# Linear attention mixed by node, graph marks in eight slots, weights and first batch norm ahead of their stages

## The chip, the cores and the metric

The kernel runs on one core of one Trainium2 chip. The metric is the device time of one execution in microseconds; lower is better. A core has five engines with an instruction queue each: TensorE (PE; PEld is its weight load), VectorE (DVE), ScalarE (ACT), GpSimd (POOL) and SyncE (SP, which here only starts DMAs). They are ordered against each other by semaphores alone. TensorE writes to eight PSUM banks of 128 x 512 f32; "bank" in a row is one of these, "arena" is the one SBUF tensor from which the kernel cuts all its tiles.

## The reference

A graph transformer of two layers on 1250 nodes with 512 features and 40000 edges. Cut to what matters here:

```python
xn = layernorm(x)
x = x + gnn0(xn, src, dst) + mix0(xn)        # layer 0; then experts
xn = layernorm(x)
x = x + gnn1(xn, edges) + mix1(xn)           # layer 1; then experts

# mix: linear attention, 8 heads of 64, no softmax
q, k, v = split(xn @ Wqkv)                   # mix1: Wqkv.T
q, k = elu(q) + 1, elu(k) + 1                # mix1: relu(q), relu(k)
kv = einsum('hnd,hne->hde', k, v)            # mix1: times temperature
den = einsum('hnd,hd->hn', q, k.sum(nodes)) + 1e-6     # mix1: max(.., 100)
y = (einsum('hnd,hde->hne', q, kv) / den) @ Wout + bout

# gnn0: three layers
for i in range(3):
    x = batchnorm(x) * gamma[i] + beta[i]    # over the nodes
    agg = segment_sum((x * src_norm)[src], dst) * dst_norm
    x = relu(agg @ W[i] + b[i])
```

All is f32. `src_norm` and `dst_norm` are inverse roots of the degrees, at least 1.

## The kernel before, in words

Nodes are cut into ten tiles of 125 (`NT`, `TS`), features into four blocks of 128 (`KT`). `st.turned` holds the normed features with features on the partitions (4 x 1250 columns), `st.res3` the residual with nodes on the partitions. The program is a list of stages; each is a block in which every engine has its own instruction list, with a barrier of all engines at its end. In layer 0 they are setup, layer norm, mixing, adjacency, graph, experts; in layer 1 layer norm, mixing, two rounds of attention on the graph, experts.

**Setup** (L112): edges and x are loaded by SP; VectorE makes from source and target two numbers for each edge: `st.low`, the place of the source in its tile, and `st.key`, target times ten plus the source's tile. `st.bound` has, for each window of 50 targets, the first and last group of four edge chunks that it needs.

**Layer norm** (L258): statistics on VectorE, root on ScalarE, scaling on VectorE, four transposes a tile on TensorE (L300), copy to `st.turned` on ScalarE. SP does nothing.

**Mixing** (`stage_mix`, L314, called once a layer; `relu` tells the second layer). SP loads the weights at its start. In layer 1 they come in rows and are turned, 16 blocks of 128 x 512, by TensorE (L395) and ScalarE (L464). Then keys and values of each node tile are made (L429, nodes on the PSUM partitions), VectorE and ScalarE shape the keys (L520, L479, L523), ScalarE copies the values (L474), and `kv_pair` (L410) adds keys times values, with a column of ones in the values that yields the sums of the keys. Queries are made the other way round, features on the partitions, in pieces of 500, 500 and 250 nodes (L425). Then for each of twelve pieces TensorE multiplies queries by the masked keys times values (L444) and by the spread sums (L445); VectorE takes the reciprocal of all of the latter (L556) and multiplies (L558). At last ten tiles are multiplied by the output weights (L454) and VectorE adds them to the residual (L563), behind the bias, which GpSimd adds to the residual (L385). In layer 0 GpSimd first makes `st.low_marks` (L382): for each of 320 chunks of 125 edges a 125 x 125 matrix in bf16 of zeros and ones; and VectorE takes the batch norm's statistics of the first graph layer (L498).

**Adjacency** (`stage_adjacency`, L572). For each of 25 windows, a loop with bounds in registers goes over its groups of four chunks: VectorE makes four marks of 125 x 500 in bf16 (L613) into four slots, TensorE multiplies each by the low marks (L637) into the window's bank, with one semaphore wait for each mark on both engines. ScalarE copies the counts (L647) and sums them. There are 104 groups. SP meanwhile zeroes two tables in memory.

**Graph** (`stage_graph`, L659). SP loads the first weights and the parameters; TensorE turns the latter (L768). For each layer the batch norm's moments (L721), root (L822) and factors (L724 to L730), the scaling of X in four pieces of 1250 columns (L733), ten products (L777), scaled by ScalarE (L825), then twelve aggregated pieces of 40 matmul records or fewer (L795), scaled (L752) and passed through relu (L834). Statistics of a feature block (L715) are taken once its three pieces are there.

## Time and profile before

| what | us |
|---|---|
| median of three runs | 2692.89 |
| lowest, highest | 2692.82, 2703.66 |
| the profiled execution | 2696.6 |
| its span, first to last instruction | 2694.8 |
| TensorE busy | 2270.1 |
| VectorE busy | 971.8 |
| ScalarE busy | 501.8 |
| GpSimd busy | 442.6 |
| mean granted TensorE clock | 0.935 |

The layer-0 stages, by the timeline: layer norm 27.1 to 43.3, mixing 43.5 to 271.8, adjacency to 457.6, graph to 871. The second mixing is at 1318.3 to 1542.4. How to read the rows below: in the busy time by stretch, a row has the stretch, its length, then for PE, PEld, DVE, ACT and POOL the busy time with the count of instructions, the granted TensorE clock (1.00 is 2.4 GHz, 0.50 is 1.2 GHz), the busy share of the DMA engines and GB/s. In the timeline a row has start, length, engine, line, operation, output <- inputs and shape, count of merged instructions, and in brackets how long the engine was idle before and what ended that. In the groups a row has the busy time, the mean length of one in ns, and the idle time before. An f32 matmul has two records.

### The profile page before, as it was taken

What the parts mean: (1) busy time and instruction counts of PE and PEld (TensorE: products, weight loads), DVE (VectorE), ACT (ScalarE), POOL (GpSimd) and SP (SyncE); (2) the same over time, 40 slices, a digit from 0 to 9 for tenths busy, and PEclk for the clock granted to TensorE, in tenths of its full rate; (3) what the DMA queues carried; (4) which work ended last, traced back from release to release, by engine and by line L of the source; (5) the groups of instructions that cost most, each with busy time, mean ns of one, the idle gap of its engine ahead of it and who ended that gap; (6) DMA issues with size and microseconds to landing.
All of it is one profiled execution on the core that took longest, in us unless ns stands there. A gap on an engine that the chain in (4) does not pass through costs nothing. (4 is left out here: it accounts for less than half of the span.)

```text
span 2694.8 us, 27626 instructions
## 1 busy us (share of the span) xinstructions
PE 2270.1 (84%) x7356; PEld 1284.5 (48%) x7357; DVE 971.8 (36%) x2322; ACT 501.8 (19%) x885; POOL 442.6 (16%) x599
## 2 busy tenths in 40 slices
PE   4976775989897898877498698998989988889996
PEld 2532332444444445444244246883458854435553
DVE  4162665420203632211105435531245402624443
ACT  1110122101010302222200014421134302201111
POOL 3995000000000014444100000000000010002332
PEclk9987998999999999999698898998999999989998
DMA  3000200000000326666300000002000010237774
GB/s 109 0 0 0 87 0 16 16 1 16 0 0 0 125 64 161 149 154 134 105 0 0 30 25 1 1 1 85 1 0 1 0 35 22 96 129 207 233 233 126
DMA packets 77350, 159.33 MB, mean 59 GB/s; under 512 B 9219, under 2 KB 20526, under 8 KB 77202
## 3 DMA queue, kind: packets, MB, share of 16 engines
q1 hardware_dynamic: 59602, 115.62, 12.8%
q0 software_dynamic: 17664, 42.64, 7.9%
q8 instruction: 47, 0.77, 0.1%
q14 instruction: 37, 0.30, 0.0%
HBM read 122.06 MB, written 38.74 MB: 60 GB/s over the span
## 5 line engine op out<-in xcount | busy, mean ns | idle before, releaser
L1692 PE MATMUL bank<-arena 125*125 125x257 f32 x1600 | 355.8, 383 | 4.8 <-DVE arena L1611 4.8
L1692 PEld LDWEIGHTS bank<-arena 125*125 125x125 f32 x1600 | 302.2, 189 | 60.5 <-DVE arena L1611 6.3
L1930 PE MATMUL bank<-arena 128*128 x832 | 250.9, 452 | 25.4 <-issue 12.6
L795 PE MATMUL bank<-arena 125*128 125x500 f32 (+1 forms) x720 | 252.6, 512 | 2.3 <-ACT arena L825 2.3
L1930 PEld LDWEIGHTS bank<-arena 128*128 128x128 f32 x832 | 157.0, 194 | 141.3 <-issue 81.8
L1507 PE MATMUL bank<-arena 128*125 128x512 f32 x480 | 211.3, 600 | 9.1 <-DMA arena<-in_L_gnn_W 9.1
L1948 PE MATMUL bank<-arena 128*128 x360 | 177.3, 622 | 36.3 <-ACT arena L1976 27.9
L795 PEld LDWEIGHTS bank<-arena 125*128 125x128 f32 x720 | 135.8, 189 | 120.5 <-issue 110.6
L382 POOL TENSOR_SCALAR arena<-arena 125x125 bf16<-125x125 f16 x320 | 184.4, 760 | 40.7 <-POOLq L266 40.7
L2022 DVE TENSOR_TENSOR arena<-bank,arena 128x384 f32<-128x384 f32 (+1 forms) x104 | 51.5, 496 | 307.8 <-PE bank L1930 296.2
L637 PE MATMUL bank<-arena 125*125 125x500 bf16 x416 | 122.8, 418 | 45.7 <-DVE arena L613 45.7
L1670 ACT ACTIVATE arena<-arena 125x625 f32<-125x625 f32 x160 | 134.5, 900 | 102.5 <-DVE arena L1611 102.3
L429 PE MATMUL bank<-arena 128*125 128x512 f32 x320 | 143.6, 603 | 10.0 <-DMA arena<-in_L_mix_Wqkv 9.3
L1507 PEld LDWEIGHTS bank<-arena 128*125 128x125 f32 x480 | 90.7, 191 | 123.3 <-issue 113.3
L1869 POOL DMA_INDIRECT token_sums<-arena x76 | 121.2, 1595 | 156.8 <-DMA token_sums<-arena 111.9
L613 DVE TENSOR_SCALAR arena<-arena 125x500 bf16<-125x500 f16 x416 | 119.0, 346 | 59.9 <-PE bank L637 53.7
L1611 DVE SCALAR_TENSOR_TENSOR arena<-arena 125x625 f32<-125x625 f32 x160 | 132.4, 864 | 15.8 <-ACT arena L1670 15.8
L777 PE MATMUL bank<-arena 128*125 128x512 f32 x240 | 111.6, 627 | 21.6 <-DVE arena L733 21.6
L752 DVE TENSOR_TENSOR arena<-bank,arena 128x500 f32<-128x500 f32 (+1 forms) x36 | 21.3, 592 | 291.7 <-PE bank L795 291.7
L1543 DVE CUSTOM_DVE_ANT_0 arena<-arena 125x256 f32<-125x256 f32 x160 | 58.6, 421 | 185.7 <-ACT arena L1530 169.3
L1044 POOL MEMSET arena<- 125x20 f32 (+1 forms) x2 | 0.2, 117 | 740.0 <-POOLq L266 740.0
L1739 POOL TENSOR_TENSOR arena<-arena 125x5120 f32<-125x5120 f32 x1 | 11.0, 10999 | 636.5 <-DMA arena<-in_L_gnn_bfc 636.5
(313 smaller groups left out, 2462.8 us busy)
## 6 DMA issues: line engine op xcount, KB each, us to landing
arena<-in_L_ffn_expert_w SPq DMA_DIRECT2D x16, 1536.0 KB
arena<-in_L_ffn_re_w SPq DMA_DIRECT2D x32, 512.0 KB
arena<-in_L_ffn_expert_w SPq DMA_DIRECT2D x16, 768.0 KB
arena<-in_L_ffn_expert_b SPq DMA_DIRECT2D x16, 384.0 KB
token_rows<-arena SPq DMA_DIRECT2D x2, 2500.0 KB
token_sums<-arena SPq DMA_DIRECT2D x20, 250.0 KB
arena<-in_L_gnn_W SPq DMA_DIRECT2D x1, 4096.0 KB, 13.1
arena<-in_L_mix_Wqkv SPq DMA_DIRECT2D x3, 1024.0 KB, 5.3
```

What stands on the lines that cost most here:

```text
L382: pool.tensor_scalar(st.low_marks[:, c, :], st.iota16[:, 0:TS], st.low[:, c:c + 1], None, ALU.is_equal)
L429: last = pe.matmul(out[0:TS, :], st.turned[:, k, i * TS:(i + 1) * TS], w3[:, k, j * D:(j + 1) * D], start=(k == 0), stop=(k == KT - 1))
L613: dve.tensor_scalar(marks[:, u, :], st.iota16[:, 0:WIN * NT], float(w * WIN * NT), st.key[:, bass.ds(col, 1)], ALU.add, ALU.is_equal).then ...
L637: pe.matmul(bank, stays, marks[:, u, :], start=False, stop=False, skip_group_check=True).then_inc(marks_free, 1)
L795: last = pe.matmul(st.bank[4 + n % 4][:, 0:cn], h[:, s, f * P:(f + 1) * P], st.counts[:, s, c0:c0 + cn], start=(s == 0), stop=(s == NT - 1))
L1507: last = pe.matmul(st.bank[n % 4][0:TS, :], x, w[:, k, half * 512:(half + 1) * 512], start=(k == 0), stop=(k == K - 1))
L1611: dve.scalar_tensor_tensor(out=prob[:, u % 2, s, :], in0=excess[:, n % EXCESS, :], scalar=by_one[:, s, head:head + 1], in1=st.counts16[:, ...
L1670: act.activation(excess[:, n % EXCESS, :], row[:, head, d0:d0 + HALF], ACT.Relu, scale=by_fifth[:, s, head:head + 1], bias=minus_one[:, s, ...
L1692: return pe.matmul(st.bank[n % OUTS][0:TS, 0:ONCOL], prob[:, u % 2, s, j * TS:(j + 1) * TS], st.slots[:, head + 1, s, :], start=(s == 0), ...
L1869: pool.indirect_dma_start(out=sums, out_offset=bass.IndirectOffsetOnAxis(ap=own_row[b][:, 0:1].bitcast(mybir.dt.uint32), axis=0), in_=y[b] ...
L1930: last = pe.matmul(st.bank[UP[b][h]][:, 0:WP], xt[b][:, k, :], rt.ring[:, bass.ds(r, 1), k * W + h * WP:k * W + (h + 1) * WP].rearrange("p ...
L1948: last = pe.matmul(st.bank[DOWN[b]], ht[b][:, f, :], rt.ring[:, bass.ds(r, 1), W2_AT + f * D:W2_AT + (f + 1) * D].rearrange("p a n -> p (a ...
```

## The change

- Mixing: all of keys, values and queries are made by node, with nodes on the partitions. GpSimd sums the keys over the tiles; one matmul with ones spreads the sums to all partitions. Keys times values (values as weights) are masked and multiplied by the output weights to one matrix `m` of 512 x 512. For each query tile VectorE multiplies by the key sums, reduces each head to one denominator, takes the reciprocal of 8 columns and scales the queries; TensorE turns the tile (4 transposes) and multiplies it by `m`; VectorE adds the result to the residual.
- The mixing's weights are loaded by SP in the layer norm stage (`mix_weights`, `load`). In layer 1, eight raw blocks are turned before the first product, eight more behind the first eight key and value tiles.
- The low marks are made by VectorE, 32 in each key tile, and not by GpSimd.
- Adjacency: eight slots of marks, used in halves of four, with one wait and one release for each group; the first graph weights are loaded here by SP, and ScalarE applies the first batch norm here. Its factors are worked out on VectorE during the mixing.
- Graph: the parameters are loaded and turned in setup; X is scaled in five pieces of 250 columns; statistics are taken piece by piece; ScalarE takes its bias straight from the parameters.

```diff
+    def load(sp):
+        for j in "kvqo":
+            c = "qkvo".index(j)
+            if turned_in:
+                rows = (wout if j == "o" else wqkv[c * D:(c + 1) * D, :]).rearrange("(r p) k -> p r k", p=P)
+                sp.dma_start(mw.raw[:, c * KT:(c + 1) * KT, :], rows).then_inc(mw.loaded[j], 16)
+            else:
+                to = mw.wo if j == "o" else mw.w3[:, :, c * D:(c + 1) * D]
+                rows = wout if j == "o" else wqkv[:, c * D:(c + 1) * D]
+                sp.dma_start(to, rows.rearrange("(k p) n -> p k n", p=P)).then_inc(mw.loaded[j], 16)
...
         @block.gpsimd
         def _(pool):
-            if not relu:
-
-                for c in range(NCH):
-                    pool.tensor_scalar(st.low_marks[:, c, :], st.iota16[:, 0:TS], st.low[:, c:c + 1], None,
-                                       ALU.is_equal)
+            for t in range(NT):
+                pool.wait_ge(ready["k"], t + 1)
+                if t == 0:
+                    pool.tensor_copy(key_sum, keys[:, 0, :]).then_inc(key_added, 1)
+                else:
+                    pool.wait_ge(key_added, t)
+                    pool.tensor_tensor(key_sum, key_sum, keys[:, t % 2, :], ALU.add).then_inc(key_added, 1)
             pool.wait_ge(b_loaded, 16)
             pool.tensor_tensor(st.res3, st.res3, bcast_mid(brow, NT), ALU.add).then_inc(res_biased, 1)
...
+            def result(t):
+                pe.wait_ge(turned_placed, t + 1)
+                if t:
+                    pe.wait_ge(y_added, t)
                 for k in range(KT):
-                    last = pe.matmul(st.bank[4 + t % 2][0:TS, :], ot[:, k, t * TS:(t + 1) * TS], wo[:, k, :],
+                    last = pe.matmul(st.bank[OUT_AT][0:TS, :], turned[:, t % 2, k, 0:TS], m[:, k, :],
                                      start=(k == 0), stop=(k == KT - 1))
                 last.then_inc(y_ready, 1)
...
+            for t in range(NT):
+                product(2 * t)
+                product(2 * t + 1)
+                if t >= 1:
+                    kv_pair(t - 1)
+                if relu and t < len(raws) - FIRST:
+                    turn_raw(FIRST + t)
+            product(NK)
+            kv_pair(NT - 1)
+            pe.wait_ge(key_added, NT)
+            pe.matmul(st.bank[SUMS][0:TS, :], st.ones[0:TS, 0:TS], key_sum, start=True, stop=True).then_inc(sums_ready, 1)
+            product(NK + 1)
...
+            pe.wait_ge(kv_masked, PAIRS)
+            for p in range(PAIRS):
+                if p >= 2:
+                    pe.wait_ge(m_placed, p - 1)
+                pe.matmul(st.bank[TURN + p % 2], kv[:, p, :], wo[:, p, :], start=True, stop=True).then_inc(m_made, 1)
+            turn(0)
+            for t in range(2, NT):
+                product(NK + t)
+                result(t - 2)
+                turn(t - 1)
+            result(NT - 2)
+            turn(NT - 1)
+            result(NT - 1)
...
+                open_product(2 * t, t)
+                if not relu:
+
+                    for c in range(t * MARKS_A_TILE, (t + 1) * MARKS_A_TILE):
+                        dve.tensor_scalar(st.low_marks[:, c, :], st.iota16[:, 0:TS], st.low[:, c:c + 1], None, ALU.is_equal)
...
+            for t in range(NT):
+                n, b = NK + t, t % 2
+                heads = lambda ap: ap.rearrange("p (h d) -> p h d", h=HEADS8)
+                open_product(n, NT + t)
+                if t == 3:
+                    dve.wait_ge(res_biased, 1)
+                if t >= 3:
+                    add_result(t - 3)
+                if t >= 2:
+                    dve.wait_ge(scaled_ready, t - 1)
+                close_product(n, NT + t, queries[:, b, :], ready["q"])
+                dve.wait_ge(ready["q"], t + 1)
+                if t == 0:
+                    dve.wait_ge(sums_ready, 1)
+                dve.tensor_tensor(weighted, queries[:, b, :], st.bank[SUMS][0:TS, :], ALU.mult).then_inc(den_step, 1)
+                dve.wait_ge(den_step, 4 * t + 1)
+                dve.tensor_reduce(den[:, b, :], heads(weighted), AX_X, ALU.add).then_inc(den_step, 1)
...
                     with dve.Fori(lo, hi, 1) as g:
                         n = dve.snap(made)
+                        half = dve.snap((n % 2) * GROUP)
+                        dve.wait_ge(marks_free, n + 1)
                         for u in range(GROUP):
-                            dve.wait_ge(marks_free, n * GROUP + (u + 1))
-                            col = g * GROUP + u
-                            dve.tensor_scalar(marks[:, u, :], st.iota16[:, 0:WIN * NT], float(w * WIN * NT),
-                                              st.key[:, bass.ds(col, 1)], ALU.add, ALU.is_equal).then_inc(marks_ready, 1)
+                            last = dve.tensor_scalar(
+                                marks[:, bass.ds(half + u, 1), :].rearrange("p a n -> p (a n)"), st.iota16[:, 0:WIN * NT],
+                                float(w * WIN * NT), st.key[:, bass.ds(g * GROUP + u, 1)], ALU.add, ALU.is_equal)
+                        last.then_inc(marks_ready, 1)
                         dve.reg_add(made, made, 1)
...
                     with pe.Fori(lo, hi, 1) as g:
                         n = pe.snap(used)
+                        half = pe.snap((n % 2) * GROUP)
+                        pe.wait_ge(marks_ready, n + 1)
                         for u in range(GROUP):
-                            pe.wait_ge(marks_ready, n * GROUP + (u + 1))
                             stays = st.low_marks[:, bass.ds(g * GROUP + u, 1), :].rearrange("p a n -> p (a n)")
-                            pe.matmul(bank, stays, marks[:, u, :], start=False, stop=False,
-                                      skip_group_check=True).then_inc(marks_free, 1)
+                            last = pe.matmul(bank, stays, marks[:, bass.ds(half + u, 1), :].rearrange("p a n -> p (a n)"),
+                                             start=False, stop=False, skip_group_check=True)
+                        last.then_inc(marks_free, 1)
                         pe.reg_add(used, used, 1)
...
+            for k in range(KT):
+                act.activation(st.turned[:, k, :], st.turned[:, k, :], ACT.Identity, scale=st.graph_scale[:, k:k + 1],
+                               bias=st.graph_shift[:, k:k + 1])
...
+                    for c0 in range(0, NODES, PW):
+                        for k in range(KT):
+                            last = dve.tensor_scalar(X[:, k, c0:c0 + PW], X[:, k, c0:c0 + PW], scale[:, k:k + 1],
+                                                     shift[:, k:k + 1], ALU.mult, ALU.add)
+                        last.then_inc(x_ready, 1)
```

## Rows read from the trace of the kernel before

**Rows 1.** Busy time by stretch: first mixing, adjacency, start and divide of the second
```profile
43.50:130.00 86.50, 78.20 (x232) 38.73 (x233) 19.86 (x33) 13.45 (x21) 85.93 (x150) 0.96 0.15 52
...
166.00:218.00 52.00, 29.52 (x48) 12.81 (x48) 39.71 (x25) 7.38 (x13) 52.00 (x92) 0.68 0.00 0
218.00:271.80 53.80, 39.41 (x80) 16.64 (x80) 6.92 (x11) 0.00 (x0) 21.43 (x20) 0.84 0.00 0
271.80:457.60 185.80, 134.54 (x466) 61.43 (x466) 120.01 (x419) 34.69 (x125) 0.00 (x0) 0.97 0.09 32
...
1318.30:1338.00 19.70, 12.46 (x64) 8.93 (x64) 0.07 (x1) 9.29 (x16) 0.00 (x0) 0.83 0.72 226
...
1451.50:1505.00 53.50, 29.49 (x48) 13.11 (x48) 46.58 (x37) 0.00 (x0) 0.00 (x0) 0.65 0.00 0
```
**Rows 2.** Timeline, start of the first mixing
```profile
43.55 8.59 SPq L371 DMA_DIRECT2D arena<-in_L_mix_Wqkv  x3
...
51.80 15.41 PE L429 MATMUL bank<-arena 128*125 128x512 f32 x32 [9.28 <-DMA arena<-in_L_mix_Wqkv]
```
**Rows 3.** Timeline, one key-value pair, two products, one reciprocal
```profile
105.86 1.06 PE L410 MATMUL bank<-arena 125*128 125x129 f32 x8
...
106.75 7.03 PE L429 MATMUL bank<-arena 128*125 128x512 f32 x16
...
170.57 3.28 DVE L556 RECIPROCAL arena<-arena 128x500 f32<-128x500 f32 x1 [4.04 <-ACT arena L488]
```
**Rows 4.** Timeline, bias on GpSimd and the output product behind it
```profile
228.14 11.30 POOL L385 TENSOR_TENSOR arena<-arena 125x5120 f32<-125x5120 f32 x1
...
240.21 22.35 PE L454 MATMUL bank<-arena 128*125 128x512 f32 x45 [13.01 <-DVE arena L563]
```
**Rows 5.** Timeline, small operations of VectorE in setup
```profile
8.42 0.93 DVE L195 TENSOR_SCALAR arena<-arena 128x25 f32<-128x25 f32 x6
...
14.11 0.47 DVE L218 TENSOR_REDUCE arena<-arena 25x80 f32<-25x320 f32 x1
```
**Rows 6.** Groups of the page: both kinds of marks
```profile
L382 POOL TENSOR_SCALAR arena<-arena 125x125 bf16<-125x125 f16 x320 | 184.4, 760 | 40.7 <-POOLq L266 40.7
...
L613 DVE TENSOR_SCALAR arena<-arena 125x500 bf16<-125x500 f16 x416 | 119.0, 346 | 59.9 <-PE bank L637 53.7
```
**Rows 7.** Adjacency: timeline of three groups, then TensorE's queue by line (ns min/median/max)
```profile
323.98 1.13 PE L637 MATMUL bank<-arena 125*125 125x500 bf16 x4 [0.20 <-DVE arena L613]
...
326.61 1.17 PE L637 MATMUL bank<-arena 125*125 125x500 bf16 x4 [1.02 <-DVE arena L613]
327.98 1.15 PE L637 MATMUL bank<-arena 125*125 125x500 bf16 x4 [0.20 <-DVE arena L613]
...
327.20 1.13 DVE L613 TENSOR_SCALAR arena<-arena 125x500 bf16<-125x500 f16 x4 [0.36 <-PE bank L637]
...
L637 PEldq FUSED_REGOPS  x416: 64/64/84, 274.1 to 451.9; - x139
...
L632 PEldq COMPARE_BRANCH  x104: 76/208/246, 275.2 to 452.1; - x104
```
**Rows 8.** Timeline, start of the graph stage
```profile
458.29 0.47 SPq L699 DMA_DIRECT2D arena<-in_L_gnn_gamma  x1
...
469.92 30.02 PE L777 MATMUL bank<-arena 128*125 128x512 f32 x64 [5.63 <-DVE arena L733]
```
**Rows 9.** Timeline, between first and second graph layer
```profile
594.94 1.58 DVE L715 BATCH_NORM_STATS2 arena<-arena 128x6 f32<-128x418 f32 x3 [0.57 <-ACT arena L834]
...
598.32 3.45 DVE L733 TENSOR_SCALAR arena<-arena 128x1250 f32<-128x1250 f32 x4
...
601.92 37.46 PE L777 MATMUL bank<-arena 128*125 128x512 f32 x80 [8.01 <-DVE arena L733]
```
**Rows 10.** Timeline, second mixing: a turned weight block placed, the last add
```profile
1325.59 0.59 ACT L464 COPY arena<-bank 128x512 f32<-128x512 f32 x1 [0.27 <-PE bank L395]
...
1541.67 0.69 DVE L563 TENSOR_TENSOR arena<-arena,bank 125x512 f32<-125x512 f32 x1 [2.75 <-PE bank L454]
```

## What the change does to the time: the prediction

> **What bounds the kernel now.** I read the busy time by stage first, then the timeline at the start, middle and end of each stage that the change touches, then the instructions that TensorE's queue runs in the adjacency loop. The first table has the stretches that the edits touch [rows 1]. In the key and value part TensorE is the bound: 78.2 us busy in 86.5. In the divide part (166 to 218) VectorE is: 39.7 us busy, mostly reciprocals of 3.28 us for 500 columns [rows 3], while TensorE gets a granted clock of 0.68. The output part (218 to 271.8) has 39.4 us of TensorE in 53.8, because its third tile waits 13.01 us, in the end for GpSimd, which makes marks until 228.14 and then adds the bias for 11.30 us [rows 4]. The second mixing has the same divide part (53.5 us) and opens with 19.7 us in which 16 weight blocks are turned. The graph stage opens at 457.6 and its first product goes at 469.92 [rows 8].
>
> **Mixing, first layer.** A product of one node tile takes 3.43 us (16 matmul records in 7.03), a key-value pair 0.88, one pass pair of 512 columns 0.86 [rows 3]. The weights now travel during layer norm. The first product started at 51.80, 8.25 us after the issue at 43.55 [rows 2]; now about 0.3 us after the stage opens. The first 32 records took 15.41 us where two times 7.03 would be 14.1; I keep 1.5 us for this start at the lower clock. From the stage's start, on TensorE:
> - wait 0.3, slow start 1.5, 20 products 68.8, 9 pairs 7.9: 78.5
> - query tile 0, last pair, key sums, query tile 1 (3.44 + 0.88 + 0.86 + 3.44): 87.1
> - four matmuls fold output weights into keys times values, 4 x 0.86, and 0.7 until the last is placed: 91.3; first turn 0.45: 91.7
> - rounds 2 to 9 are a product, a result and a turn: 3.44 + 3.44 + 0.45 = 7.33. From round 3 on there is a new wait. result(t-2) needs y_added of the tile before; VectorE adds that one only behind open_product(t), which needs the product that TensorE has just ended. So each round TensorE stands for a semaphore (0.2), the min of 0.6 (0.69 with its end overlapped), the add of 0.69 [rows 10], and the way back 0.06: 1.55. One round of 7.33 and seven of 8.88: 161.2
> - last result, turn, placing and add, result, add (3.44 + 0.45 + 0.8 + 3.44 + 0.9): 170.2
> With 0.4 for the barrier the stage takes 170.6 instead of 228.3 us: **57.5 us gone**. The 52 us of dividing go nearly whole, as reciprocals act on 8 numbers a node; against them stand 3.4 us of folding, 4.5 of turns and 10.9 of the new wait.
>
> **Does VectorE keep up?** Its 320 marks are new there. No row shows a 125-wide mark on VectorE. On GpSimd, 320 took 184.4 us, 0.58 apart [rows 6]. A 500-wide mark starts every 0.26 us on VectorE (four in 1.13 with the last one's 0.35 in it); a 25-wide operation with a per-partition scalar every 0.14 (six in 0.93) [rows 5, 6]. Between these, by width, lies 0.165, and I take it, as the 500-wide ones are the same operation. A tile then costs 0.2 + 0.6 + 32 x 0.165 + 0.69 = 6.8 us under TensorE's 7.75; the cover left is 1 us, and it is gone at 0.195 a mark. Tile 0 opens late (statistics, square root, reciprocal: 7.8 us in), but its keys are wanted only behind product 3, at 15.7. In the query rounds VectorE has open, add, close, multiply by the sums (0.6 to 0.7 each), a reduce of 512 (from 0.47 for 320 [rows 5]: 0.67), two operations on 8 columns (0.17 each) and the scaling 0.7: 4.5 us, under 8.9. Scaled(t-1) is wanted 11 us behind its product. GpSimd adds keys once a tile (1.2 us by [rows 4], 5120 columns in 11.30) and the bias at about 83 to 95 us, wanted at 103.
>
> The Trainium skill, "VectorE: DVE Perf Modes", section "Mode 2×_1P — pack two bf16 into one 32-bit read", asks for 4-byte alignment of packed 16-bit data, and every second mark row starts 250 bytes on. By it half the marks would fall to about 0.26, 8.3 us a tile and some 6 us more (a part of B below). Its page "Vector Engine (DVE) Microarchitecture Reference", section 5.1, says that alignment makes no difference. No row of the kernel before decides.
>
> **Mixing, second layer.** Here the raw weights are loaded in layer norm and eight blocks are turned before the first product, 0.86 each, as now (0.59 of copy and 0.27 of wait [rows 10]): products start 7.7 us in, not 19.7. The other eight blocks ride behind the key and value tiles, 0.45 us of TensorE each. 7.7 + 1.5 + 68.8 + 7.9 + 3.6 = 89.5; 8.6 to 98.1; 4.1 to 102.3; 0.45 and 7.33 to 110; rounds 3 to 9 have no min before the add, so the wait is 0.2 + 0.69 + 0.06 = 0.95: 7 x 8.28 to 168; tail 9.0: 177. The stage took 224.1 (1318.3 to the last add [rows 10]): **47 us gone**.
>
> **Adjacency.** The alternation TensorE, VectorE, TensorE in the waits looks like a lack of slots, and eight slots would cure that. But the queue rows say otherwise [rows 7]. Groups start 1.37 us apart (326.61, 327.98); the four matmuls of one take 1.15 to 1.17. For each matmul TensorE's queue runs a register instruction of 64 ns with the wait (416 of them), and a group closes with a compare and branch of 208 ns. These are serial. The first mark of the group at 327.98 is begun at 327.20 and done, at 0.35 a mark, at 327.55, 0.43 before its matmul; the fourth is begun 0.79 behind it and done 0.35 before the fourth matmul starts at about 328.7, less a way of 0.1. So I take TensorE's queue as the bound, and more slots give it nothing. The edit takes out three of four waits and the add that makes each one's value, and puts in a second computed address for each matmul and the half of the group. Matmuls of a group start 0.24 apart ((1.15 - 0.42) / 3). If all of a matmul's arithmetic fits into one register instruction, this falls to what 500 bf16 columns take, by estimate half of the 0.43 of an f32 record of 512 [rows 3], 0.1 us a group; if it needs two, it grows to 0.26 and the group's head by 0.1, 0.2 us a group. 104 groups: 10 us less to 21 more. I take 0, the middle being +3. The first batch norm on ScalarE lies in its idle 9 us before the first window, the load of the graph weights at the head of SP's queue lies beside 186 us.
>
> **Graph stage.** Weights, parameters and the first scaling are done when it opens, so its first product goes at 458.2 and not at 469.92 [rows 8]: **11.7 us gone**. The 23 us reduce of VectorE moves forward with it by 10 and still ends before tile 7. Between layers the last statistics are one piece (0.4) and not three (1.58), and the first product needs four scalings of 250 columns (1.3 us) and not 3.45 [rows 9]: 1.2 + 2.1 = 3.3, twice: **6.6 us gone**.
>
> **Setup.** SP issues three small parameter loads ahead of x, which the stage waits for: 0.47, 0.4, 0.4 [rows 8]: **1.3 us more**.
>
> **Sum.** -57.5 - 47 + 0 - 11.7 - 6.6 + 1.3 = -121.5. The profiled execution took 2696.6 us (span 2694.8) and would take 2575; it lies 3.7 above the median of the runs, 2692.9, so the median comes to 2571.
>
> **Rivals.**
> - B, the marks run at the pace of one element a cycle, 0.26 (bound: a 500-wide mark). VectorE needs 9.8 us a tile and has keys 9 at 7.8 + 98 = 106 where TensorE wants them at 82: +23, **2594**. For: no row shows a 16-bit operation of this odd width; against: 500-wide marks take half of that for each column. 0.10
> - C, the address arithmetic of the adjacency loop needs two register instructions on either queue: +25, **2596**. For: the queue is the bound and each matmul gets one more address. 0.13
> - D, the query rounds are not TensorE's: TensorE waits for VectorE's whole chain (4.5 us, not 1.55 or 0.95) because of the shared order: +3 x 14 = 42, **2613**. Against: scaled(t-1) has 11 us. 0.08
> - F, the lockstep of four slots does cost: with it gone a group takes 1.28 and half of each of 25 window changes is hidden: -22, **2549**. For: every second row of the waits names the other engine. 0.11
> - S, slower than before: the half of the group, n modulo 2, is lowered to something like a window change, which costs 2.63 - 1.37 = 1.3 us [rows 7], in each of 104 groups: +135, **2706**. It decides from 2.5 us a group on. Against: both numbers are in registers. 0.02
> - The change does not do what it says (weights not there, folding no shorter), all edits together giving nothing: 0.01.
>
> **How the numbers follow.** The forecast case has 0.55, 2558 to 2584 by itself. From F to C lie 0.89 of the chance; I set 2546 to 2604. A measurement here tells some 0.5% from no change, 13 us. Faster 0.97, same 0.01, slower 0.02.
>
> **What would show it.** Right: the first product of both mixings within 1 and 8 us of the stage; TensorE idle 1.5 and 0.95 us before each result, put down to VectorE's add; 32 marks in about 5.3 us; groups 1.3 to 1.45 apart; graph stage with its first product in 0.5 us. Wrong: marks apart by 0.2 or more, a wait of TensorE for keys, two register instructions a matmul, gaps ahead of the turns.

## The result and the profile after

The changed kernel takes **2608.22 us** (median of four runs, 2606.02 to 2611.35); the kernel before, measured beside it, 2697.06 (2692.82 to 2703.66). The ratio is 0.9674, 95% interval 0.9654 to 0.9695: 88.8 us less. The forecast was 121.5 less (2571, range 2546 to 2604). The profiled execution took 2606.02 us, its span is 2604.2, against 2696.6 and 2694.8: 90.6 less. The stage times in this section compare these two profiled executions.

Four lines of the changed kernel's busy time by stretch, one each for the first mixing, the adjacency, the graph stage and the second mixing (busy us and instructions of each engine, TensorE's granted clock, DMA share, GB/s):

```profile
43.10:224.90 181.80, 161.46 (x450) 75.42 (x450) 124.52 (x444) 27.73 (x46) 22.97 (x11) 0.97 0.01 2
224.90:440.70 215.80, 151.87 (x466) 64.16 (x466) 119.52 (x419) 40.05 (x129) 0.00 (x0) 0.92 0.09 32
440.70:844.60 403.90, 371.83 (x1006) 189.42 (x1006) 104.72 (x170) 47.45 (x74) 0.00 (x0) 0.96 0.02 6
1282.10:1457.00 174.90, 164.84 (x514) 80.49 (x514) 47.36 (x86) 22.58 (x40) 21.37 (x11) 1.00 0.01 2
```

The stage times beside those of [rows 1, 8, 10], and what the prediction gave each:

| part | before | after | gain | predicted |
|---|---|---|---|---|
| first mixing | 228.3 | 181.8 | 46.5 | 57.5 |
| adjacency | 185.8 | 215.8 | **-30.0** | 0 |
| open of the graph stage to its first product | 12.3 | 0.1 | 12.2 | 11.7 |
| from there to the first transpose of layer norm (879.90 before, 844.65 after) | 410.0 | 403.9 | 6.1 | 6.6 |
| second mixing | 224.1 | 174.9 | 49.2 | 47 |
| setup | | | 0 | -1.3 |
| all the rest, same program | | | 6.6 | 0 |

So four of the terms are right within 2.2 us, and two are not: the first mixing by 11, the adjacency by 30. The rest, whose program is the same but for the loads that moved into it, came out 6.6 us shorter; that is no more than the runs of one kernel differ among themselves (2692.8 to 2703.7 before).

**The parts that came as told.** Timeline of the changed kernel (start us, duration, engine, line, operation, count, idle time before and what ended it) at the open of the first mixing, the open of the graph stage, a layer boundary, and the open of the second mixing:

```profile
43.15 13.97 PE L443 MATMUL bank<-arena 128*125 128x512 f32 x32 [1.09 <-PEq L277]
50.77 5.30 DVE L594 TENSOR_SCALAR arena<-arena 125x125 bf16<-125x125 f16 x32
...
440.80 5.45 PE L863 MATMUL bank<-arena 128*125 128x512 f32 x6 [5.24 <-PEq L669]
...
568.32 6.49 DVE L820 TENSOR_SCALAR arena<-arena 128x250 f32<-128x250 f32 x20
569.84 10.55 PE L863 MATMUL bank<-arena 128*125 128x512 f32 x17 [4.70 <-DVE arena L820]
...
1282.19 3.69 PE L426 MATMUL bank<-arena 128*128 128x128 f32 x32 [1.09 <-PEq L277]
...
1286.92 1.55 PE L443 MATMUL bank<-arena 128*125 128x512 f32 x3 [1.05 <-ACT arena L516]
```

The first product goes with the stage, where it stood 9.28 us for its weights [rows 2], and at the full clock (1.00 granted from 43.1 to 57; 13.97 us for 32 records, so the slow start of 1.5 us that I kept is not there). The 32 marks take 5.30 us, 0.163 apart, where 0.165 was taken. The graph's first product starts 0.1 us behind the stage; between layers TensorE stands 4.70 and not 8.01 us [rows 9]: 3.3, as told. In the second mixing products start 4.8 us in, not the 7.7 forecast: the eight copies of turned blocks take 4.01 us, 0.50 each, where the forecast had 0.86 each from a stretch with a granted clock of 0.83 (here it is 1.00) and loads still under way. Which of the two made the difference no run tells apart. The earlier start, 2.9 us, is more than the 2.2 us by which the whole stage beat its forecast.

**Where the first mixing lost 11 us.** The same timeline where keys times values become folded weights:

```profile
123.62 11.00 POOL L407 TENSOR_TENSOR arena<-arena 125x5120 f32<-125x5120 f32 x1
...
128.09 0.69 DVE L638 TENSOR_REDUCE arena<-arena 125x8 f32<-125x512 f32 x1
128.56 1.88 PE L499 MATMUL bank<-arena 128*128 128x512 f32 x4
128.81 5.83 DVE L640 TENSOR_SCALAR arena<-arena 125x8 f32<-125x8 f32 x1
134.68 0.20 DVE L643 RECIPROCAL arena<-arena 125x8 f32<-125x8 f32 x1
...
136.78 1.05 ACT L549 COPY arena<-bank 128x512 f32<-128x512 f32 x2
...
137.40 3.78 PE L499 MATMUL bank<-arena 128*128 128x512 f32 x4 [6.96 <-ACT arena L549]
...
141.95 1.07 PE L463 MATMUL bank<-arena 125*128 125x125 f32 x4 [0.77 <-ACT arena L549]
142.81 5.11 PE L443 MATMUL bank<-arena 128*125 128x512 f32 x8
...
209.88 0.68 DVE L576 TENSOR_TENSOR arena<-arena,bank 125x512 f32<-125x512 f32 x1
210.71 3.67 PE L472 MATMUL bank<-arena 128*125 128x512 f32 x8 [1.47 <-DVE arena L576]
```

GpSimd adds the bias from 123.62 to 134.62. VectorE's operation on 8 columns, 0.17 us elsewhere, is held from 128.81 to 134.64, though it shares no data with that add. Behind it on VectorE stands the opening of query tile 1, on ScalarE that tile's exponential, and behind the exponential the copies that place the folded weights: TensorE stands 6.96 us and starts again at the lower clock (0.50 granted from 137.4 to 142 and 0.52 from 142 to 146; 5.11 us for 8 records and not 3.60). The last two lines are the new wait of the query rounds, 1.47 us where 1.55 was told.

**Where the adjacency lost 30.** Timeline of four groups, then TensorE's queue by line (ns min/median/max, first and last start):

```profile
397.11 1.23 PE L727 MATMUL bank<-arena 125*125 x4 [0.39 <-issue]
398.69 1.13 DVE L700 TENSOR_SCALAR arena<-arena 125x500 f16 x4 [0.49 <-PE bank L727]
398.75 1.23 PE L727 MATMUL bank<-arena 125*125 x4 [0.40 <-issue]
...
400.38 1.23 PE L727 MATMUL bank<-arena 125*125 x4 [0.40 <-issue]
...
402.01 1.23 PE L727 MATMUL bank<-arena 125*125 x4 [0.40 <-issue]
...
404.93 1.27 PE L727 MATMUL bank<-arena 125*125 x4 [1.24 <-DVE arena L700]
...
L727 PEldq FUSED_REGOPS  x832: 60/74/141, 228.7 to 434.8; - x167
```

Groups are 1.63 us apart (398.75, 400.38) and not 1.37 [rows 7]; a window change takes 2.92 (402.01 to 404.93) and not 2.63. The queue runs 832 address instructions where it ran 416. Within a window TensorE now waits for "issue", its own queue; VectorE is named mostly where a window changes (36.3 us in 31 waits over the loop, before 45.7 us in 99). VectorE's marks are not held back by their own second address here: the four of a group take 1.13 us, as before. That is rival C, by its own mechanism, on TensorE's side. From the first to the last weight load the loop takes 205.8 us and not 177.7.

### The profile page after: what moved, and what is told of

The parts are those of the page before. It is cut to its first block and busy times, and to the rows that moved or that the text cites. A ratio compares the mean times of both kernels' runs of the same rounds, so it can differ in the third digit from the quotient of the medians.

```text
span 2604.2 us, 27822 instructions
## 1 busy us (share of the span) xinstructions
PE 2239.5 (86%) x7328; PEld 1261.2 (48%) x7329; DVE 992.9 (38%) x2694; ACT 514.3 (20%) x900; POOL 284.8 (11%) x299
## 5 line engine op out<-in xcount | busy, mean ns | idle before, releaser
L2011 PEld LDWEIGHTS bank<-arena 128*128 128x128 f32 x832 | 157.2, 195 | 140.7 <-issue 80.8
L1588 PE MATMUL bank<-arena 128*125 128x512 f32 x480 | 211.0, 600 | 8.8 <-DMA arena<-in_L_gnn_W 8.8
L443 PE MATMUL bank<-arena 128*125 128x512 f32 x480 | 214.1, 596 | 2.1 <-PEq L277 1.1
L727 PE MATMUL bank<-arena 125*125 x416 | 140.1, 455 | 58.0 <-DVE arena L700 36.3
L700 DVE TENSOR_SCALAR arena<-arena 125x500 f16 x416 | 118.5, 347 | 89.1 <-PE bank L727 46.4
L1588 PEld LDWEIGHTS bank<-arena 128*125 128x125 f32 x480 | 90.6, 191 | 122.8 <-issue 113.2
L443 PEld LDWEIGHTS bank<-arena 128*125 128x125 f32 x480 | 87.6, 189 | 101.9 <-issue 100.6
L727 PEld LDWEIGHTS bank<-arena 125*125 x416 | 59.3, 143 | 142.5 <-issue 109.1
L863 PE MATMUL bank<-arena 128*125 128x512 f32 x240 | 112.1, 630 | 14.6 <-DVE arena L820 9.4
L2029 PEld LDWEIGHTS bank<-arena 128*128 128x128 f32 x360 | 62.6, 190 | 100.8 <-issue 100.8
```

Source lines behind the costliest of these rows:

```text
L443: last = pe.matmul(st.bank[n % 4][0:TS, :], st.turned[:, k, t * TS:(t + 1) * TS], w3[:, k, j * D:(j + 1) * D], start=(k == 0), stop=(k == ...
L700: last = dve.tensor_scalar(marks[:, bass.ds(half + u, 1), :].rearrange("p a n -> p (a n)"), st.iota16[:, 0:WIN * NT], float(w * WIN * NT), ...
L727: last = pe.matmul(bank, stays, marks[:, bass.ds(half + u, 1), :].rearrange("p a n -> p (a n)"), start=False, stop=False, skip_group_check ...
L863: last = pe.matmul(st.bank[s % 4][0:TS, :], X[:, k, s * TS:(s + 1) * TS], w[:, k, :], start=(k == 0), stop=(k == KT - 1))
L1588: last = pe.matmul(st.bank[n % 4][0:TS, :], x, w[:, k, half * 512:(half + 1) * 512], start=(k == 0), stop=(k == K - 1))
L2011: last = pe.matmul(st.bank[UP[b][h]][:, 0:WP], xt[b][:, k, :], rt.ring[:, bass.ds(r, 1), k * W + h * WP:k * W + (h + 1) * WP].rearrange("p ...
```

## The experiments

Thirteen versions ran; those measured together share their runs of the kernel before (medians 2696.25, 2695.60, 2697.18 and 2694.88). Stage times in this part run from TensorE's first instruction in one stage to its first in the next; so counted the changed kernel has 182.5 us in the first mixing, 215.2 in the adjacency, 182.9 in the second mixing.

### The bias add out of the way

The same wait and add now stand at the head of GpSimd's list in `stage_graph`; that part is not shown.

```diff
-            pool.wait_ge(b_loaded, 16)
-            pool.tensor_tensor(st.res3, st.res3, bcast_mid(brow, NT), ALU.add).then_inc(res_biased, 1)
+            if bias_here:
+                pool.wait_ge(b_loaded, 16)
+                pool.tensor_tensor(st.res3, st.res3, bcast_mid(brow, NT), ALU.add).then_inc(res_biased, 1)
...
-        stage_mix(nc, st, free, mw, ins["L0_mix_bout"])
+        stage_mix(nc, st, free, mw, ins["L0_mix_bout"], bias_here=False)
```

> The changed kernel (2608.2 us), with the bias add of the first mixing on GpSimd (one TENSOR_TENSOR over 5120 columns, 11.0 us) taken out of the mixing and put at the open of the graph stage, where VectorE runs a long reduce and GpSimd is idle. Everything is still computed. Theory H (GpSimd's add holds VectorE's operations that read and write only SBUF with one tensor input): in the changed kernel the 8-column maximum/add of query tile 0 took 5.83 us and ended with GpSimd's add; it goes back to 0.17, the fold is placed 4.6 us behind query tile 1 and not 13.4, and the product after it takes 3.4 to 3.6 us and not 4.9. The first mixing falls from 181.8 to about 171.5 us, the whole to about 2598. Rival H2 (the small chain itself is slow there, for its semaphores or its shape, and GpSimd only happens to end with it): the operation stays at 5.8 us, the mixing at 181.8, the whole at 2608. The add costs nothing at its new place by either.

Measured: 2601.39 us (2596.96 to 2602.43), ratio to before 0.9655 (0.9633 to 0.9677); first mixing 173.1 us. Its timeline:

```profile
128.29 0.17 DVE L642 TENSOR_SCALAR arena<-arena 125x8 f32<-125x8 f32 x1
...
131.22 1.98 PE L501 MATMUL bank<-arena 128*128 128x512 f32 x4 [1.29 <-ACT arena L551]
...
433.00 11.08 POOL L794 TENSOR_TENSOR arena<-arena 125x5120 f32<-125x5120 f32 x1 [309.85 <-DMA arena<-in_L_mix_bout]
```

The operation is back at 0.17 us and the stage is 9.4 shorter, as theory H said; of the whole, 6.8 show in the medians. At its new place the add lies beside VectorE's long reduce, which takes 23.5 us as before (23.4): a reduce is not held.

### The copies ahead of the exponential

```diff
             if not relu:
                 exp(NT)
-                exp(NT + 1)
             for p in range(PAIRS):
                 act.wait_ge(m_made, p + 1)
                 act.copy(m[:, p, :], st.bank[TURN + p % 2]).then_inc(m_placed, 1)
+            if not relu:
+                exp(NT + 1)
```

> The changed kernel with one move in ScalarE's list of the first mixing: the four copies that place the folded weights go ahead of the exponential of query tile 1. The hold of VectorE stays as it is. Theory Q (TensorE stands for the fold only because ScalarE's copies are queued behind an exponential whose input VectorE makes behind the held operation): the copies run at about 129 to 132 us, the first turn goes as soon as VectorE has scaled tile 0, at about 135.8 and not 141.95, and the product behind it is faster by up to 1.3: 6 to 7.5 us less, about 2601. Rival (the held operation is on the path in any order, and TensorE is as late through the scaling): under 1 us, 2607 to 2608.

Measured: 2602.37 us (2596.73 to 2607.02); first mixing 176.0 us, 6.5 less. TensorE now waits for VectorE's scaling alone:

```profile
132.00 0.58 ACT L548 COPY arena<-bank 128x512 f32<-128x512 f32 x1 [0.27 <-PE bank L499]
...
135.42 1.10 PE L463 MATMUL bank<-arena 125*128 125x125 f32 x4 [3.46 <-DVE arena L648]
```

So of the 9.4 us that moving the add gave, 6.5 (two thirds) came through ScalarE's order; the other 2.9 are the scaling that is still late here.

### The bias add first

```diff
+            if not relu:
+                pool.wait_ge(b_loaded, 16)
+                pool.tensor_tensor(st.res3, st.res3, bcast_mid(brow, NT), ALU.add).then_inc(res_biased, 1)
             for t in range(NT):
                 pool.wait_ge(ready["k"], t + 1)
...
+            if relu:
+                pool.wait_ge(b_loaded, 16)
+                pool.tensor_tensor(st.res3, st.res3, bcast_mid(brow, NT), ALU.add).then_inc(res_biased, 1)
```

> The changed kernel with GpSimd's bias add of the first mixing put ahead of its key adds, so that it runs at the open of the mixing, beside VectorE's statistics and the first marks. Theory H (GpSimd's two-input add holds VectorE's SBUF-to-SBUF operations with one tensor input): marks that should start at 50.8 stand until the add ends, about 57; keys of tile 0 come some 6 us late, and TensorE, which wants them behind four products, waits some 5 us; the hold of 5.83 us in the query part is gone with its 9.4 us. Together the first mixing takes about 177 us (181.8 as changed, 172.4 with the add moved out of the stage). If the hold were one of memory traffic in general, the statistics of 0.67 us a piece would be longer too; by H they are not, as the products by the sums and the reduce beside the add were not. Rival H2 (nothing is held): marks start at 50.8, the mixing takes 172 to 173.

Measured: 2609.75 us (one run); first mixing 181.4 us. The timeline, and below it the marks' line by itself (ns min/median/max):

```profile
43.03 6.02 DVE L587 BATCH_NORM_STATS2 arena<-arena 128x6 f32<-128x500 f32 x12 [1.82 <-PEq L277]
...
46.58 11.01 POOL L401 TENSOR_TENSOR arena<-arena 125x5120 f32<-125x5120 f32 x1 [43.20 <-DMA arena<-in_L_mix_bout]
...
50.65 12.05 DVE L598 TENSOR_SCALAR arena<-arena 125x125 bf16<-125x125 f16 x32
...
63.42 2.08 PE L455 MATMUL bank<-arena 125*128 125x128 f32 x8 [6.42 <-DVE arena L575]
...
L598 DVE TENSOR_SCALAR arena<-arena x320: 240/250/7007, 50.6 to 129.6; 125x125 bf16<-125x125 f16 x160
```

The hold goes where the add goes: one mark lasts 7.0 us, the 32 take 12.05 and not 5.30, and the statistics beside the same add take their 6.02. Theory H holds. My price for it was low (177 expected): TensorE stood 6.42 us and restarted at the lower clock (0.64 granted from 63.4 to 68), so nearly all of the gain at the old place was given back.

The small adds do the same in the changed kernel: GpSimd's key adds of 1.27 us start at 63.31, 70.44 and 77.49, and in each of them one mark lasts 0.88 to 0.90 us where the median is 0.25. Nothing of it reaches TensorE, which is busy for 60.00 of the 60 us from 60 to 120.

This agrees with the Trainium skill, "SBUF — State Buffer", section "Who interferes with whom": a copy or tensor-scalar of VectorE in a mode that uses two ports and a GpSimd instruction exclude each other for the whole length of the one that came first, and a reduce never contends. The trace shows both, 5.83 us of hold and 23.5 for the reduce. The prediction had GpSimd's add in the stage and called it harmless because its result was wanted late.

### The adjacency loop of before

TensorE's side; VectorE's list goes back likewise, to four slots.

```diff
-                        half = pe.snap((n % 2) * GROUP)
-                        pe.wait_ge(marks_ready, n + 1)
                         for u in range(GROUP):
+                            pe.wait_ge(marks_ready, n * GROUP + (u + 1))
...
-                            last = pe.matmul(bank, stays, marks[:, bass.ds(half + u, 1), :].rearrange("p a n -> p (a n)"),
+                            pe.matmul(bank, stays, marks[:, u, :], start=False, stop=False,
```

> The changed kernel with the adjacency loop of before: four slots at fixed addresses, a wait and a signal for each mark. All else is as changed (first batch norm on ScalarE and the load of graph weights in that stage, marks made in the mixing). Theory C (the second computed address costs a register instruction more for every matmul and every mark, 2 x 416 in the queues where there were 416): groups go from 1.62 back to 1.37 us, window changes from 2.92 to 2.64, and the stage from 215.7 to 187 or 188; the whole to about 2580. Rival S2 (the stage is long because it opens at a lower granted clock and with ScalarE's and SP's added work): the loop's own rows improve, but the stage stays above 195, the whole above 2588. Rival L (the eight slots did give something and the registers took more): the groups come out above 1.37.

Measured: 2580.70 us (2569.33 to 2583.27), 27.5 less; the stage 187.0 us, groups again 1.37 apart (383.38, 384.75):

```profile
383.38 1.15 PE L724 MATMUL bank<-arena 125*125 125x500 bf16 x4 [0.21 <-DVE arena L700]
...
384.75 1.15 PE L724 MATMUL bank<-arena 125*125 125x500 bf16 x4 [0.21 <-DVE arena L700]
```

The stage is 28.2 us shorter and the loop, from first to last weight load, 26.9 (178.9). The batch norm on ScalarE and the load of the graph weights in the same stage cost next to nothing: the loop takes 178.9 us with them and 177.7 in the kernel before.

### A second address on one queue alone

The kernel before with this on TensorE, and in a further version the like on VectorE:

```diff
+                        half = pe.snap((pe.snap(nil) % 2) * GROUP)
...
-                            pe.matmul(bank, stays, marks[:, u, :], start=False, stop=False,
+                            pe.matmul(bank, stays, marks[:, bass.ds(half + u, 1), :].rearrange("p a n -> p (a n)"), start=False, stop=False,
```

> The kernel before with one thing added in the adjacency loop, on TensorE alone: the slot of the marks is a computed address (from a register that holds zero, so the slots and all results stay the same), one more register instruction for each matmul, while the wait and its sum stay. In the trace of before one matmul's turn in TensorE's queue is a sum (32 ns, next start 92 on), an address with the wait (64 ns, 114 on to the weight load) and 29 to the next sum: 235 ns. In the changed kernel two address instructions take the place of sum and address: 29 + 132 + 110 = 271. Theory C (the queue is serial and bounds the loop; a register instruction costs its own time and some 58 ns more): 29 + 92 + 132 + 110 = 363 ns a matmul, 0.51 us a group, 53 us and some 10 for the group's head: about 2750 to 2760. Rival L (the loop is held by the lockstep of two engines over four slots, and the queue has air): groups stay at 1.37 to 1.45, the time under 2705.

> The kernel before with the same computed slot on VectorE's side alone: one more register instruction for each mark. VectorE's queue takes 0.22 us a mark and 1.05 us a group if nothing holds it, under the 1.37 of TensorE's queue; with the added one 0.35 a mark and 1.6 us a group. Theory C (queues are serial, the slower one bounds): VectorE's queue becomes the bound by 0.2 us, 104 groups: 15 to 25 us more, about 2715. Rival (VectorE reads its queue ahead while it computes a mark of 0.35 us, so its register work is hidden): under 5 us, 2696 to 2701.

Measured: TensorE 2765.33 us, ratio 1.0264 (1.0247 to 1.0281); VectorE 2749.87, ratio 1.0193 (1.0168 to 1.0219). First TensorE's version, then VectorE's:

```profile
344.39 1.56 PE L639 MATMUL bank<-arena 125*125 x4 [0.45 <-DVE arena L613]
...
346.40 1.56 PE L639 MATMUL bank<-arena 125*125 x4 [0.45 <-DVE arena L613]
```

```profile
349.36 1.37 DVE L615 TENSOR_SCALAR arena<-arena 125x500 f16 x4 [0.49 <-PE bank L639]
...
351.21 1.37 DVE L615 TENSOR_SCALAR arena<-arena 125x500 f16 x4 [0.48 <-PE bank L639]
```

On TensorE the weight loads of a group stand 364 ns apart (median), where 363 was worked out, and groups 2.01 us; the whole is 69.7 us slower, 5 above the top of what I expected; the group's head grew by 0.23 (from 642 to 870 ns) where I had 0.1, and the granted clock of the stage fell from 0.97 to 0.80. On VectorE marks stand 0.34 us apart (0.35 worked out), but groups 1.85 us and not 1.6, and 54 us came where 15 to 25 were expected. The row puts the 0.48 us ahead of a group's first mark down to TensorE, but the matmul that frees that slot started 1.34 us before and took 0.42, so by these times it is VectorE's own queue at the head of its loop. Either queue alone can become the bound; both of these versions have a sum beside the two addresses, which the changed kernel has not.

### One wait a group

```diff
-                            pe.wait_ge(marks_ready, n * GROUP + (u + 1))
+                            if u == 0:
+                                pe.wait_ge(marks_ready, n * GROUP + GROUP)
```

> The kernel before with one edit on TensorE's side of the adjacency loop: it waits once a group, for the fourth mark, and no longer for each, so three sums (ALU_OP) a group leave its queue; slots, addresses and VectorE's side stay. It measures two costs by themselves. Spacing of the four matmuls: by the serial queue 29 + 114 = 143 ns, unless streaming 500 columns bounds it, half of the 0.43 of an f32 record of 512, so about 210; before 235. That is the lower bound of the prediction for one register instruction a matmul. Lockstep: the group's first matmul now stands for the fourth mark, and the next marks for these matmuls, with four slots: some 0.4 (matmul) + 0.15 + 1.05 + 0.3 = 1.9 us a group and not 1.37, 104 x 0.5 = about 50 us, 2750. If groups stay under 1.45, the slots never mattered in either direction.

Measured: 2778.99 us (one run), the loop 252.5 us from first to last weight load. The address instructions of a group now follow one another in 143 ns, where a matmul's turn took 235, as the sum of the queue's parts says; the matmuls themselves do not, they start 0.42 us apart. But with four slots the engines take turns, and TensorE, which stands 0.66 us in every 2.58, runs at a granted clock of 0.63 in this stage, 0.42 us a matmul:

```profile
333.69 1.92 PE L638 MATMUL bank<-arena 125*125 125x500 bf16 x4 [0.66 <-DVE arena L613]
334.54 1.57 DVE L613 TENSOR_SCALAR arena<-arena 125x500 bf16<-125x500 f16 x4 [1.01 <-PE bank L638]
...
336.27 1.92 PE L638 MATMUL bank<-arena 125*125 125x500 bf16 x4 [0.66 <-DVE arena L613]
```

2.58 us a group where I expected 1.9: the clock was not in my sum. Three starts of 0.42 and not 0.21 us make 0.63 of the difference of 0.68.

### The residual's add ahead of the opening

```diff
-                open_product(n, NT + t)
                 if t == 3:
                     dve.wait_ge(res_biased, 1)
                 if t >= 3:
                     add_result(t - 3)
+                open_product(n, NT + t)
```

> The changed kernel with two lines of VectorE exchanged in the query rounds of both mixings: the add of result t-3 to the residual goes ahead of the opening of query tile t, not behind it. Theory W (TensorE stands in each round only because the add that frees the result's bank is queued behind an operation that needs the product TensorE has just ended): the waits of 1.47 us in the first mixing and 0.87 in the second go, seven each, as the result before was ready long ago: 10.3 + 6.1 = 16.4 us less, about 2592. Rival W2 (the wait moves on to the turn, because the scaled tile or the placing is late once the round is 7.4 us): under 6 us less, 2602 or more. The chain of VectorE is 4.5 to 5.4 us a round, so I expect W.

Measured: 2590.04 us (2585.88 to 2596.54), 18.2 less; 11.2 in the first mixing and 7.3 in the second. The rounds are 7.30 us long and have no wait, but for the last two results (1.68 and 0.67 us):

```profile
176.32 3.60 PE L472 MATMUL bank<-arena 128*125 128x512 f32 x8
179.75 0.59 PE L463 MATMUL bank<-arena 125*128 125x125 f32 x4
180.18 3.60 PE L443 MATMUL bank<-arena 128*125 128x512 f32 x8
183.62 3.60 PE L472 MATMUL bank<-arena 128*125 128x512 f32 x8
```

The wait that the prediction priced at 1.55 and 0.95 us a round came from the order of two lines.

### The weights loaded late

```diff
-        stage_layernorm(nc, st, Arena(whole, mid, words), load=mw.load)
+        stage_layernorm(nc, st, Arena(whole, mid, words))
...
         def _(sp):
+            mw.load(sp)
             if relu:
```

> The changed kernel with one part undone: the weights of both mixings are issued at the open of the mixing, as before, and not in layer norm (in the same order and pieces). The prediction gave the early load 8 us in the first mixing (first product 0.3 and not 8.25 us behind the open) and a part of 12 in the second. Theory: the first product of the first mixing goes 8 us later, TensorE has no other work there; in the second the first turned block goes 8 us later; and the first products start at the lower clock, 1.3 us each: about 17 to 19 us more, 2625 to 2627. Rival (the loads only trade places with other traffic and VectorE's statistics and marks bound the start of the first mixing): 8 to 10 us, 2617.

Measured: 2620.67 us (2619.60 to 2624.97), 12.5 more than the changed kernel. The first product of the first mixing goes at 48.95, 5.8 us later and not 8.

```profile
48.95 3.77 PE L444 MATMUL bank<-arena 128*125 128x512 f32 x4 [6.30 <-DMA arena<-in_L_mix_Wqkv]
```

It waits for the keys' megabyte alone, where the kernel before waited for keys and values, two, before its first product; so the 8.25 us of [rows 2] were no price of this order. The direction is right, the size some 5 us under my 17 to 19.

### All mended, and eight slots without a second address

The four edits together (bias add moved, copies first, the loop of before, the add first), then with the loop's wait by pairs, then with a loop over two groups, then with both. In the loop over two groups a window with an odd number of groups takes one more, which has no marks in it; the padding for it is not shown.

> The changed kernel with four edits together: the bias add of the first mixing moved to the graph stage, the copies of the folded weights ahead of an exponential, the adjacency loop of before, and the residual's add ahead of the opening of the next query tile. Apart they gave 6.8 (9.3 in the profiled stage), 5.9 (6.5), 27.5 and 18.2 us. The first two cure the same stall, so one of them counts: 9.4 + 28 + 18.5 = 56, about 2552. If the edits share more than that (the rounds of 7.3 us find VectorE late once marks or scaling are close, or the clock falls where TensorE has no pauses), 2560 to 2575.

```diff
-                            pe.wait_ge(marks_ready, n * GROUP + (u + 1))
+                            if u % 2 == 0:
+                                pe.wait_ge(marks_ready, n * GROUP + (u + 2))
```

> The mended version (2552.9) with one more edit in the adjacency loop: TensorE waits for two marks at a time, so two of three sums a group leave its queue. By the serial queue the second and fourth matmul start 143 to 210 ns behind the one before and not 235, the pair's first one waits for a mark that VectorE makes 0.26 us later than the first. If TensorE's queue is the bound by itself: 104 x 0.05 to 0.18 = 5 to 19 us less, 2534 to 2548. If VectorE's marks (four slots, freed by matmul) are as near: the same, 2550 to 2556, or slower.

```diff
+    STEP = 2 * GROUP
...
-                    with pe.Fori(lo, hi, 1) as g:
+                    with pe.Fori(lo, hi, 2) as g:
                         n = pe.snap(used)
-                        for u in range(GROUP):
-                            pe.wait_ge(marks_ready, n * GROUP + (u + 1))
+                        for u in range(STEP):
+                            pe.wait_ge(marks_ready, n * STEP + (u + 1))
```

> The mended version (2552.9) with a loop that takes two groups, eight chunks, an iteration: eight slots, all at fixed addresses, a wait for each mark; a window with an odd number of groups takes one group more, which has no mark in it (about 58 iterations and 464 matmuls where there were 104 groups and 416; a padding group at the end). It gives eight slots without the second address. By TensorE's serial queue an iteration is 8 x 0.235 + 0.42 = 2.3 us, 58 x 2.3 and 25 window changes at 1.29 more: 166 us from first to last weight load, where it was 178.6: 12 us less, 2541. If the lockstep of four slots had cost something beside the queue, the spacing of matmuls, now 236 to 240 ns, can't fall below 235, so nothing more comes. If VectorE bounds (0.26 a mark, 8 x 0.26 + 0.44 = 2.5 us an iteration): 58 x 0.2 more, 178, the same as now.

> As the version before in this set (two groups an iteration, eight slots at fixed addresses), and TensorE waits for two marks at a time, so four of seven sums leave its queue. With four slots this edit gave nothing (the stage 186.2 against 186.8). Theory B (with four slots two bounds lay at the same height, the queue of TensorE and the round from a matmul over the freed slot to the next mark; taking away either alone gives nothing, both together does): the iteration falls to what VectorE's marks take, 8 x 0.26 and a head of 0.2 to 0.4, 2.3 to 2.4 us at most, or TensorE's 4 x 0.143 + 3 x 0.235 + 0.62 = 1.9: 58 x 2.1 to 2.3 and 32 for the windows: 154 to 165 us, 1 to 12 less than with single waits. Rival (the queue of TensorE alone counted, and slots never): 1.9 us an iteration, 142, 24 less. If it is the same as with single waits, VectorE's marks are the bound.

| version | us (lowest to highest) | ratio to before | adjacency | loop |
|---|---|---|---|---|
| all mended | 2552.94 (2546.41 to 2556.94) | 0.9468 (0.9452 to 0.9485) | 186.8 | 178.6 |
| ... waits by pairs | 2556.94 (2550.22 to 2562.30) | 0.9480 (0.9463 to 0.9498) | 186.2 | 177.8 |
| ... two groups, eight slots | 2535.06 (2532.59 to 2539.77) | 0.9410 (0.9392 to 0.9428) | 167.1 | 158.9 |
| ... two groups, waits by pairs | **2524.59** (2519.18 to 2526.16) | 0.9362 (0.9343 to 0.9381) | 157.6 | 149.1 |

The mended version came at 2552.9 where 2552 was expected, with the two cures of one stall counted once: the effects add.

Two groups an iteration take 2.32 us, as the serial queue says (2.3), and the 432 matmuls are fewer than the 464 I had counted. Of the loop's 19.7 us hardly any is the slots': matmuls of an iteration start 235 ns apart where they started 240 apart, at most 2 us in all. The gain is that of fewer iterations. The gaps between iterations and windows take 65.3 us (53 of them) and not 100.5 (103), the spacings inside an iteration 93.6 us (378) and not 78.1 (312).

With four slots, fewer sums in TensorE's queue gave nothing (0.6 us of the stage): the spacings inside a group fell from 240 to 148 ns in the median, and the gap ahead of the next group, within a window, rose from 643 to 706. With eight at fixed addresses the same edit gave 9.5. So with four slots two bounds lay at one height, the queue and, as these numbers read it, the round from a matmul over its freed slot to the next mark. With both edits, marks and matmuls flow without a gap inside a window:

```profile
289.90 4.28 DVE L706 TENSOR_SCALAR arena<-arena 125x500 bf16<-125x500 f16 x16 [1.17 <-PE bank L731]
290.96 4.01 PE L731 MATMUL bank<-arena 125*125 125x500 bf16 x16 [1.02 <-DVE arena L706]
```

Sixteen marks in 4.28 us, 0.26 apart, where VectorE made four every 1.37 us before. This version is 83.6 us under the changed kernel and 170 under the one before.

## Why the prediction missed

1. **Adjacency, taken at 0 of -10 to +21: wrong by 30, four fifths of the miss.** The step that failed is the value, not the mechanism. TensorE's queue was named as the bound, and the prediction said that two register instructions a matmul would add 0.2 us a group; they added 0.25 (the spacing went from 236 to 271 ns, three times, 0.11, and the head from 642 to 790, 0.15), and 0.27 where a window changes (2.66 to 2.93 in the median): 104 times, 28. I then took 0 between two cases that exclude each other (the middle of -10 and +21 is +5.5, not the +3 written there). Each operand with a computed address costs an instruction of its own: the edit takes out a sum of 32 ns and puts in one of 60 to 74. The sign of being wrong that I had named, two register instructions a matmul, is there. Rival C is what came; by it the sum was 2596.
2. **"More slots give it nothing": right for the queue as it was.** With a second address eight slots cost 28 us. At fixed addresses the version with them is 17.9 us faster, but by its fewer iterations and not by the slots (235 for 240 ns a matmul). Only with a lighter queue did the slots count: the edit that gave nothing with four gave 10.5 us with eight. Rival F, in which four slots cost with the queue unchanged, did not come: a window change takes 1.93 us from its last weight load to the next with eight slots, 1.95 with four.
3. **First mixing, 57.5 taken, 46.5 measured.** The start came 1.7 us better; from the second query product to the first turn it took 13.4 us and not 4.2, the product behind it 1.5 more, and the rounds and the tail 2 more. The failing step is "GpSimd adds ... the bias at about 83 to 95 us, wanted at 103": it asked only when the result is wanted, not what runs beside it. Its time was right: 80 to 91 us behind the stage's open.
4. **The waits of the rounds** (1.47 for 1.55; 0.87 for 0.95), the marks (0.163 for 0.165), VectorE under TensorE's pace, the first products, the layer boundary and the open of the graph stage: as told, in place and size. Rivals B, D and S did not come.
5. **Second mixing:** 49.2 for 47, through a start at 4.8 us and not 7.7, less what the rest gave back. The same add holds VectorE there too, but the small operation takes 0.92 us there, 0.75 more, since the add ends soon (at 1375.93). It is off the path: TensorE's first turn waits for the copies of the folded weights, ahead of which no exponential stands in this layer.
6. **Setup:** 1.3 us more told, none measured: layer norm opens at 27.07, before at 27.08. No run was made on why.
7. The rule weighed there on 4-byte alignment of 16-bit data (the Trainium skill, "VectorE: DVE Perf Modes", section "Mode 2×_1P — pack two bf16 into one 32-bit read"; by it 8.3 us a tile and 6 more in all) is not borne out: marks start 0.163 us apart in the median, alike for the rows at a multiple of 4 bytes and for those 250 bytes on, as its page "Vector Engine (DVE) Microarchitecture Reference", section 5.1, has it.

The total was 37 us off: 41 by points 1 and 3, less 3.5 by the other terms and 6.6 by the rest, and 6 by the way from the profiled run to the median (3.7 taken off, as before, where the changed kernel's median lies 2.2 above its profiled run).

## What to carry to other kernels

In a loop bound by an engine's queue, price an edit in register instructions. On TensorE here each took its own time and 50 to 60 ns more (a sum 32 ns, the next start 92 on; an address 64 ns, the weight load 114 on), and each operand with a computed address had one. Unrolling over two fixed halves bought more slots without them, and half the iterations besides. Where two unlike cases span a term, forecast the likelier one, not the middle. For every long two-input operation on GpSimd ask which copies and tensor-scalars of VectorE run beside it, and what other engines have queued behind these.

## What the runs showed that I had not expected

- A GpSimd add of 11.0 us held a VectorE operation of 0.17 us for 5.83, and a mark for 7.0. Statistics (6.02 us for 12), a reduce of 23.5 us and a product with one operand in the accumulators (0.69) ran beside it unheld.
- The parts of TensorE's queue add up: 235, 271, 364 and 143 ns a matmul (medians) for a sum and an address, two addresses, a sum and two addresses, and an address alone. 363 and 143 had been worked out before their runs.
- Two bounds at one height hide each other: lightening the queue gave 0.6 us of the stage with four slots and 9.5 with eight.
- Half the iterations were worth more than the slots: 19.7 us of the loop, of which 2 at most are the slots'.
- An alternation of the engines costs twice: TensorE stood 0.66 us a group, and at the lower clock its four matmuls took 1.92 us where they take 1.15.
